# Scatters of routed rows spread over the batches, with a third buffer of rows and indices

## The chip, the cores and the metric

The kernel runs on one core of a Trainium2 chip. The metric is device time in microseconds of one execution, from three runs: 939.26, 940.46 and 940.62, median 940.46. A run with the hardware profiler on gives the trace that is read below.

## The reference

One decoder layer over 64 batches of 128 tokens with 128 features, in float32:

```python
x = src + linear_attention(layer_norm(src)); x = x + gelu(layer_norm(x) @ w1 + b1) @ w2 + b2
x = x + cross_attention(layer_norm(x), ctx)              # 16 heads of 8, 77 keys for each batch
probs = softmax(layer_norm(x) @ gate_w.T)                # 8 experts, each token takes the top 2
rank = cumsum(one_hot(top_i), axis=0) - 1                # rank of a token at its expert, over all 8192 tokens
keep = rank < capacity                                   # 1280 rows for each expert and choice
x = x + sum over kept choices of weight * down(silu(gate(z)) * up(z))   # z = layer_norm(x)
```

(Shortened: biases and the fill of masked keys are left out.)

## The kernel before

It has three stages. The first does linear attention and the feed-forward part. The second (`cross_attention_and_routing`, about 260 to 690 us) does cross-attention and finds for every token its two experts and a row in each. The third (`experts_and_combine`) loads the rows of one expert after another, computes, and scatters the results.

**Turns.** The second stage works on 16 groups of four batches (NG = 16, G4 = 4; a batch is one tile of 128 tokens). Every engine has its own hand-written program: a loop over turns g from 0 to 18, and in each turn four steps j = 0 to 3, one for each batch b = 4g + j. Work is pipelined over turns. In turn g TensorE does the attention of group g, the out-projection of group g-1 (`project_out`), the transposes of group g-1's normalised rows (`t4`, L1363), the gate of group g-2 and its ranks. Scores (L1303) and their maxima (`tops`, L933, two halves for each batch) run two batches ahead.

**GpSimd's steps.** For batch b+2 `split_top` (L811 and L813) writes the maxima as a high and a low part into Mx. TensorE transposes them one batch later (`turn_top`, L1308). `ln_scale` (L821 to L826) makes the scale and shift of the third norm for group g+2 in step 0 and of the fourth norm for group g-1 in step 2; `add_out_bias` (L831) follows in step 2. In between stand the scatters.

**Scatters.** `scatter_rows` (L834) is an indirect DMA: 128 rows of one tile, from z4 to the DRAM tensor `dispatched` of choice k, at the rows that `idx` holds. A row holds the normalised features, the residual and five numbers. Each group has four tiles and two choices, so eight scatters. In turn g, step 3, GpSimd waits for `residual_ready` and `idx_ready` of group g-2 and scatters tile 0 (both choices). In the next turn, tiles 1 and 2 go around the split of step 0 and tile 3 behind the split of step 1. For the last two groups (14 and 15) the first choice of all tiles goes first, then the second.

**Who waits for the scatters.** z4 and idx have two buffers. ScalarE (`ln4_apply`, L1197 and L1198, step 2) writes group g-1's rows and first waits until the scatters of group g-3 have landed. Behind it on ScalarE's queue stand the exponentials of the next batch (`exps`, L1215), for which TensorE waits before L1308. VectorE waits in step 13 of `route`. SyncE waits for all first-choice scatters before the first `load_x` (xin) of the third stage, and for all second-choice scatters before its second half.

**The order at the end.** Turns 14 and 15 have no third norm left to scale, turn 16 has no attention of its own, and its step 2 holds the fourth norm's scale of group 15.

Of the kernel before, what the change touches and what calls it, by code (L numbers as in the profile page):

```python
# [16 lines left out]
P = 128  # L17
# [26 lines left out]
NO_TOKEN = float(2 ** 20)  # L44
TOKENS = P * B


# [4 lines left out]
def some(count):  # L52

    return not isinstance(count, int) or count > 0
# [635 lines left out]
def cross_attention_and_routing(nc, ctx, sems, d, X, ident, neghalf, psum, banks, xg, c):  # L690
# [5 lines left out]
    if True:  # L696
        def sb(name, shape, dt=F32):
            return ctx.enter_context(nc.sbuf_tensor(name, shape, dt))

        def sem(name):  # L700
# [29 lines left out]
        var4, rs4, shift4 = (sb(n, [P, G4]) for n in ("var4", "rs4", "shift4"))  # L730
        z4 = [sb(f"z4{i}", [P, G4, ROW]) for i in range(2)]
        z4T = sb("z4T", [P, G4 * P])
# [10 lines left out]
        rank, row, drop = (sb(n, [P, G4, K2]) for n in ("rank", "row", "drop"))  # L743
        idx = [sb(f"idx{i}", [P, G4, K2], I32) for i in range(2)]

# [4 lines left out]
                 "ln4_stats ln4_moments ln4_var ln4_rstd ln4_shift z4_ready z4T_ps z4T_ready gate_ps dl_ready ex_ready "  # L750
                 "rank_ps ranked_ready residual_ready idx_ready step scattered0_0 scattered1_0 scattered0_1 scattered1_1").split()
        s = {n: sem("b_" + n) for n in names}
# [38 lines left out]
        def gpsimd(pool):  # L791
# [40 lines left out]

            def scatter_rows(par, t, k):
                pool.indirect_dma_start(xg[k], bass.IndirectOffsetOnAxis(ap=idx[par][:, t, k:k + 1], axis=0), z4[par][:, t, :], None,  # L834
                                        bounds_check=E * CAP - 1, oob_is_err=False).then_inc(s[f"scattered{par}_{k}"], 16)

            def scatter(g, par, t):
                if t == 0:
                    pool.wait_ge(s["residual_ready"], g + 1)
                    pool.wait_ge(s["idx_ready"], g + 1)  # L840
                    pool.sem_inc(s["passed"], 1)
                if not isinstance(g, int) or g < NG - 2:
                    for k in range(K2):
                        scatter_rows(par, t, k)

                elif t == 0:
                    for u in range(G4):
                        scatter_rows(par, u, 0)
                elif g == NG - 2:
                    if t == 1:  # L850
                        scatter_rows(par, 0, 1)
                        scatter_rows(par, 1, 1)
                else:
                    for u in range(2):
                        if t == 1:
                            scatter_rows(1 - par, 2 + u, 1)
                        else:
                            scatter_rows(par, 2 * (t - 2) + u, 1)

            def steps(g, par):  # L860
                other = 1 - par
                for j in range(G4):
                    b = G4 * g + j
                    if j == 0:
                        if group(g + 2):
                            ln_scale(g + 2, 3, mom3, var3, rs3, shift3)
                        if group(g - 3):
                            scatter(g - 3, other, 1)
                    if j == 2:
                        if group(g - 1):  # L870
                            ln_scale(g - 1, 4, mom4, var4, rs4, shift4)
                        if group(g):
                            add_out_bias(g)
                    if batch(b + 2):
# [33 lines left out]
        def vector(dve):  # L908
# [85 lines left out]
            def route(g, par, k):  # L994
# [44 lines left out]
                if k == 13:  # L1039
                    if some(g - 1):  # L1040
                        for k in range(K2):
                            dve.wait_ge(s[f"scattered{par}_{k}"], 16 * G4 // 2 * (g - par))

                    v.tensor_scalar(taken[:], rank[:, :, 1], float(CAP), None, ALU.is_lt)
                    v.tensor_scalar(z4[par][:, :, ALONE], rank[:, :, 1], float(CAP), None, ALU.is_ge)
# [6 lines left out]
                if k == 15:  # L1052
                    v.tensor_tensor(z4[par][:, :, PLACE], away[:], codes[:, bass.ts(g, G4)], ALU.add)
                    ins = v.reciprocal(z4[par][:, :, WEIGHT], pair[:])
                if k == 16:
                    ins = v.tensor_tensor(z4[par][:, :, WEIGHT + 1], z4[par][:, :, WEIGHT], ex[:, :, E], ALU.mult)
                ins.then_inc(s["step"], 1)

            def indices(g, par):
                dve.wait_ge(s["step"], STEPS * g + STEPS)  # L1060
                v.scalar_tensor_tensor(idx[par][:], row[:], float(ROWS), drop[:], ALU.add, ALU.add).then_inc(s["idx_ready"], 1)

# [118 lines left out]
        def scalar(act):  # L1181
# [7 lines left out]

            def ln4_apply(g, par, t):  # L1190
                if t == 0:
                    act.wait_ge(s["ln4_shift"], g + 1)
                    if some(g - 1):
# [3 lines left out]
                    nc.scalar.activation(z4[par][:, :, CODE:CODE + 1], codes[:, bass.ts(g, G4)].unsqueeze(2), ACT.Copy)  # L1197
                ins = nc.scalar.activation(z4[par][:, t, 0:P], xrow(g, t), ACT.Identity, bias=shift4[:, t:t + 1], scale=rs4[:, t:t + 1])  # L1198
                if t == G4 - 1:
                    ins.then_inc(s["z4_ready"], 1)  # L1200
# [6 lines left out]

            def residual_side(g, par):
                nc.scalar.activation(z4[par][:, :, X_AT:X_AT + P], X[:, bass.ts(g, G4), :], ACT.Copy).then_inc(s["residual_ready"], 1)

# [25 lines left out]
            def steps(g, par):  # L1236
                other = 1 - par
                for j in range(G4):
                    b = G4 * g + j
                    if batch(b):  # L1240
                        exps(b, j)
                    if batch(b - 1):
                        num_out(b - 1)
                    if batch(b + 1):
                        MT_side(b + 1)
                    if j == 1 and group(g + 2):
                        ln3_apply(g + 2)
                    if j == 2:
                        if group(g - 2):
                            gate_exps(g - 2)  # L1250
                        if group(g - 1):
                            for t in range(G4):
                                ln4_apply(g - 1, other, t)
                    if j == 3 and group(g - 1):
                        z4T_side(g - 1)
                        residual_side(g - 1, other)

# [16 lines left out]
        def tensor(pe):  # L1274
# [84 lines left out]

            def t4(g, par):  # L1360
                pe.wait_ge(s["z4_ready"], g + 1)
                for t in range(G4):
                    last = nc.tensor.transpose(misc[:, t * P:(t + 1) * P], z4[par][:, t, 0:P], ident[:])  # L1363
                last.then_inc(s["z4T_ps"], 1)
# [19 lines left out]
            def steps(g, par):  # L1384
# [3 lines left out]
                for j in range(G4):  # L1388
# [47 lines left out]
                    if j == 3 and group(g - 1):  # L1436
                        if group(g + 2):
                            pe.wait_ge(s["z3T_ready"], g + 3)
                        else:
                            pe.wait_ge(s["ranked_ready"], g - 1)  # L1440
                        t4(g - 1, other)

# [58 lines left out]
def experts_and_combine(nc, ctx, sems, d, X, ident, psum, banks, xg, out):  # L1501
# [6 lines left out]
    if True:  # L1508
# [54 lines left out]
        def sync(sp):  # L1563
            def load_x(n, i, p):
# [4 lines left out]
                if n == SECOND:  # L1569
                    for par in (0, 1):  # L1570
                        sp.wait_ge(b[f"scattered{par}_1"], 16 * G4 * NG // 2)
                slot = n // SECOND
# [45 lines left out]
            for g in range(NG - 2, NG):  # L1618
                store_x(g)
            for par in (0, 1):  # L1620
                sp.wait_ge(b[f"scattered{par}_0"], 16 * G4 * NG // 2)
            load_x(0, 0, 0)
# [222 lines left out]
```

## Time and profile before

| | |
|---|---|
| Median of three runs | 940.46 us |
| The profiled execution | 943.81 us, of which the span of the trace is 942.0 us |
| TensorE busy | 860.0 us, 91% of the span |
| VectorE busy | 652.4 us, 69% |
| GpSimd busy | 538.7 us, 57% |
| ScalarE busy | 449.4 us, 48% |
| Scatters of the second stage (L834) | 128, busy 129.5 us, mean 1012 ns |
| GpSimd idle ahead of L811, waiting for the maxima | 108.6 us, 36 times |

Engines in rows: PE is TensorE's matmuls, PEld its weight loads, DVE VectorE, ACT ScalarE, POOL GpSimd, SP SyncE; a q behind a name is the engine's sequencer. Matmuls overlap and their ends are modelled. Ln is line n of the kernel. An arrow `out<-in` names tiles by the program's names without their numbers; "z" stands for z4 too. A releaser in square brackets is what ended the idle time before an instruction. "issue" means that the profile shows nothing it waited for.

### The profile page before, as it was taken

What the parts mean: (1) busy time and instruction counts of PE and PEld (TensorE: products, weight loads), DVE (VectorE), ACT (ScalarE), POOL (GpSimd) and SP (SyncE); (2) the same over time, 40 slices, a digit from 0 to 9 for tenths busy, and PEclk for the clock granted to TensorE, in tenths of its full rate; (3) what the DMA queues carried; (4) which work ended last, traced back from release to release, by engine and by line L of the source; (5) the groups of instructions that cost most, each with busy time, mean ns of one, the idle gap of its engine ahead of it and who ended that gap; (6) DMA issues with size and microseconds to landing.
All of it is one profiled execution on the core that took longest, in us unless ns stands there. A gap on an engine that the chain in (4) does not pass through costs nothing.

```text
span 942.0 us, 25271 instructions
## 1 busy us (share of the span) xinstructions
PE 860.0 (91%) x9107; PEld 614.8 (65%) x9107; DVE 652.4 (69%) x2060; ACT 449.4 (48%) x695; POOL 538.7 (57%) x747
## 2 busy tenths in 40 slices
PE   3799999999989999999999999997449999989994
PEld 2577777777656666666666666665327777657672
DVE  5789989999736688888888888764415555464553
ACT  1267566675435666666666666654122223322330
POOL 3356666566432236656666666653646666657775
PEclk9799999999989999999999999987569999999997
DMA  7269930000000001111000000010143545456660
GB/s 242 89 233 403 402 152 0 0 0 2 1 1 2 14 26 59 59 60 41 32 28 29 31 29 29 30 47 24 39 149 110 159 126 157 121 173 194 197 196 7
DMA packets 50335, 86.99 MB, mean 92 GB/s; under 512 B 12809, under 2 KB 28105, under 8 KB 50232
## 3 DMA queue, kind: packets, MB, share of 16 engines
q1 hardware_dynamic: 37872, 72.18, 22.6%
q0 software_dynamic: 11264, 12.70, 4.2%
q8 instruction: 66, 1.08, 0.5%
q10 hardware_dynamic: 1096, 0.73, 0.2%
q14 instruction: 37, 0.30, 0.1%
HBM read 42.08 MB, written 58.41 MB: 107 GB/s over the span
## 4 chain that ended last, share of the span: by engine, by line
PE 50%; POOL 7%; issue 6%; DVE 5%; ACT 5%; DMA 2%; POOLq 0%; SPq 0%; DVEq 0%; ACTq 0%
PE psum L1743 14%; PE psum L1755 7%; PE psum L1303 6%; PE psum L1317 4%; PE psum L1337 4%; POOL dispatched L834 3%; ACT PT L1215 2%; PE psum L1737 2%; ACT z L1198 2%; PE psum L1357 2%; PE psum L1345 2%; PE psum L1287 1%; POOL rs L824 1%; PE psum L1370 1%; PE psum L625 1%
## 5 line engine op out<-in xcount | busy, mean ns | idle before, releaser
L1642 POOL DMA_INDIRECT out<-yo,token x160 | 157.6, 985 | 82.8 <-issue 70.4
L834 POOL DMA_INDIRECT dispatched<-z,idx x128 | 129.5, 1012 | 68.5 <-issue 68.5
L1215 ACT ACTIVATE PT<-psum,key_bias 77x2048 f32<-77x2048 f32 x64 | 125.5, 1960 | 78.8 <-PE psum L1320 78.8
L1724 ACT ACTIVATE act_g<-psum 128x512 f32<-128x512 f32 x80 | 47.3, 597 | 159.7 <-PE psum L1743 137.5
L933 DVE TENSOR_REDUCE top_score<-psum 128x8 f32<-128x616 f32 x128 | 101.4, 792 | 29.1 <-PE psum L1303 25.9
L1303 PE MATMUL psum<-Kb,qT 32*128 32x308 f32 x512 | 102.3, 475 | 0.4 <-DVE top_score L933 0.4
L1680 DVE SCALAR_TENSOR_TENSOR yo<-psum,xin,base 128x128 f32<-128x128 f32 x156 | 44.0, 344 | 75.7 <-PE psum L1755 75.4
L1317 PE MATMUL psum<-qT,Kb 32*77 32x128 f32 x2048 | 86.7, 285 | 0.1
L1755 PE MATMUL psum<-down,h 128*128 128x128 f32 x640 | 78.3, 275 | 4.0 <-DVE h L1695 4.0
L1755 PEld LDWEIGHTS psum<-down,h 128*128 128x128 f32 x640 | 74.7, 192 | 5.8 <-DVE h L1695 5.3
L1743 PE MATMUL psum<-xT,gate 128*128 128x512 f32 (+1 forms) x192 | 77.1, 532 | 0.8 <-ACT xT L1715 0.8
L1743 PE MATMUL psum<-xT,up 128*128 128x512 f32 (+1 forms) x192 | 75.4, 522 | 0.0
L811 POOL CAST Mx<-top_score 128x16 bf16<-128x16 f32 x64 | 12.9, 201 | 108.6 <-DVE top_score L933 108.6
L1337 PE MATMUL psum<-PT,V 77*32 77x128 f32 x2048 | 70.9, 280 | 0.7 <-issue 0.7
L1337 PEld LDWEIGHTS psum<-PT,V 77*32 77x32 f32 x2048 | 53.3, 111 | 27.4 <-issue 27.0
L1317 PEld LDWEIGHTS psum<-qT,Kb 32*77 32x77 f32 x2048 | 60.6, 146 | 11.6 <-issue 11.0
L625 PE MATMUL psum<-w,hT 128*128 128x128 f32 x512 | 66.8, 281 | 0.8 <-ACT hT L522 0.8
L1695 DVE TENSOR_TENSOR h<-psum,act_g 128x512 f32<-128x512 f32 x80 | 54.0, 686 | 15.5 <-PE psum L1743 15.5
L625 PEld LDWEIGHTS psum<-w,hT 128*128 128x128 f32 x512 | 62.6, 197 | 1.6 <-ACT hT L522 1.6
L605 PE MATMUL psum<-ln2T,w 128*128 128x512 f32 x128 | 61.8, 605 | 0.6
L1320 PE MATMUL psum<-MT,minus_sel 32*77 32x128 bf16 x1024 | 61.0, 217 | 0.0
L1743 PEld LDWEIGHTS psum<-xT,gate 128*128 128x128 f32 x192 | 36.9, 193 | 33.5 <-issue 31.8
(173 smaller groups left out, 1744.5 us busy)
## 6 DMA issues: line engine op xcount, KB each, us to landing
dispatched<-zeros SPq DMA_DIRECT2D x40, 522.0 KB, 6.5
xin<-dispatched SPq DMA_DIRECT2D x40, 522.0 KB, 3.6
out<-zeros SPq DMA_DIRECT2D x20, 256.0 KB, 3.1
first<-out SPq DMA_DIRECT2D x20, 256.0 KB, 4.3
X<-in_x SPq DMA_DIRECT2D x16, 256.0 KB, 2.6
out<-X SPq DMA_DIRECT2D x16, 256.0 KB
out<-yo,token POOLq DMA_INDIRECT x160, 2.7
ctx<-in_ctxT SPq DMA_DIRECT2D x4, 616.0 KB, 5.8
```

Source lines behind the costliest of these rows:

```text
L605: nc.tensor.matmul(h_ps[c % 2], w1[:, c * P:(c + 1) * P], ln2T[:], start=True, stop=True).then_inc(s["h_ps"], 1)
L625: last = nc.tensor.matmul(w2_ps[:, t, :], hT[:, c, t * P:(t + 1) * P], w2[:, c, :], start=(c == 0), stop=(c == FC - 1))
L834: pool.indirect_dma_start(xg[k], bass.IndirectOffsetOnAxis(ap=idx[par][:, t, k:k + 1], axis=0), z4[par][:, t, :], None, bounds_check=E * C ...
L933: v.tensor_reduce(top_score[p][:, 2 * HB * half:2 * HB * half + 2 * HB], S, AX.X, ALU.max).then_inc(s["top_ready"], 1)
L1215: nc.scalar.activation(PT[j % 2][:], T.rearrange("p a c -> p (a c)"), ACT.Exp, bias=key_bias[:, bass.ds(b, 1)]).then_inc(s["PT_ready"], 1)
L1303: nc.tensor.matmul(S[:, i], qT[par][rows_of(q), j * P:(j + 1) * P], Kb[par][rows_of(q), :, j * S2:(j + 1) * S2], start=True, stop=True).th ...
L1317: nc.tensor.matmul(T[:, q, h * P:(h + 1) * P], Kb[par][rows_of(q), h, j * S2:(j + 1) * S2], qT[par][rows_of(q), j * P:(j + 1) * P], start= ...
L1320: last = nc.tensor.matmul(T[:, q, h * P:(h + 1) * P], minus_sel[rows_of(q), h, :], MT[rows_of(q), :], start=False, stop=True)
L1337: last = nc.tensor.matmul(pv[rows_of(q), a * P:(a + 1) * P], V[par][:, (H // 2) * j + x, ROWS_Q * i:ROWS_Q * i + ROWS_Q], PT[j % 2][:, (2 ...
L1642: pool.indirect_dma_start(rows_out if slot else out, bass.IndirectOffsetOnAxis(ap=token[i][:, t:t + 1], axis=0), yo[i][:, t, :], None, bou ...
L1743: last = nc.tensor.matmul(target[c][:, a:b], weights[which][:, c * P:(c + 1) * P], xT[i][:, a:b], start=True, stop=True)
L1755: last = nc.tensor.matmul(target, h[:, c, t * P:(t + 1) * P], down[which][:, c, :], start=(c == 0), stop=(c == HC - 1))
```

## The change

z4 and idx get three buffers (Z4 = 3); which one a group uses is g mod 3, and every wait on a buffer's scatters counts by it. Groups 0 to 13 are scattered one tile in each step, three turns behind (n = g-3): the wait for group n's residual and indices moves from step 3 of turn n+2 to step 0 of turn n+3; then in each step GpSimd waits for the first half of batch b+2's maxima, scatters the first choice of tile j, splits the maxima, and scatters the second choice. Groups 14 and 15 keep their order. The scales and the out-bias stay where they were within the steps.

```diff
+Z4 = 3
-        z4 = [sb(f"z4{i}", [P, G4, ROW]) for i in range(2)]
+        z4 = [sb(f"z4{i}", [P, G4, ROW]) for i in range(Z4)]
-        idx = [sb(f"idx{i}", [P, G4, K2], I32) for i in range(2)]
+        idx = [sb(f"idx{i}", [P, G4, K2], I32) for i in range(Z4)]
...
+            def scatter_ready(g):
+                pool.wait_ge(s["residual_ready"], g + 1)
+                pool.wait_ge(s["idx_ready"], g + 1)
+                pool.sem_inc(s["passed"], 1)
...
             def steps(g, par):
-                other = 1 - par
                 for j in range(G4):
                     b = G4 * g + j
-                    if j == 0:
-                        if group(g + 2):
-                            ln_scale(g + 2, 3, mom3, var3, rs3, shift3)
-                        if group(g - 3):
-                            scatter(g - 3, other, 1)
+                    n = g - 3
+                    paced = 0 <= n < NG - 2
+                    if j == 0 and group(g + 2):
+                        ln_scale(g + 2, 3, mom3, var3, rs3, shift3)
                     if j == 2:
                         if group(g - 1):
                             ln_scale(g - 1, 4, mom4, var4, rs4, shift4)
                         if group(g):
                             add_out_bias(g)
+                    if paced:
+                        if j == 0:
+                            scatter_ready(n)
+                        if batch(b + 2):
+                            pool.wait_ge(s["top_ready"], 2 * (b + 2) + 1)
+                        scatter_rows(n, j, 0)
+                    elif j < G4 - 1 and group(n):
+                        scatter_last(n, j + 1)
                     if batch(b + 2):
                         split_top(b + 2, j % 2)
-                    if j == 3 and group(g - 2):
-                        scatter(g - 2, par, 0)
-
-                    if j < 2 and group(g - 3):
-                        scatter(g - 3, other, j + 2)
+                    if paced:
+                        scatter_rows(n, j, 1)
+                    if j == 3 and g - 2 in (NG - 2, NG - 1):
+                        scatter_last(g - 2, 0)
...
-                    if some(g - 1):
-                        act.wait_ge(s["z4T_ps"], g - 1)
+                    if some(g // Z4):
+                        act.wait_ge(s["z4T_ps"], g - Z4 + 1)
                         for k in range(K2):
-                            act.wait_ge(s[f"scattered{par}_{k}"], 16 * G4 // 2 * (g - par))
+                            act.wait_ge(s[f"scattered{g % Z4}_{k}"], 16 * G4 * (g // Z4))
```

The wait of VectorE in step 13 of `route` and SyncE's waits change in the same way. `scatter_last` issues for groups 14 and 15 what `scatter` issued for them.

## Rows read from the trace of the kernel before

**Rows 1.** Stretches of TensorE: span, busy (instructions), granted clock, DMA share, GB/s

```profile
405.00:429.00 24.00, 23.70 (x425) 1.00 0.14 50
...
453.00:547.00 94.00, 93.81 (x1624) 1.00 0.09 28
...
626.00:628.00 2.00, 0.79 (x13) 1.00 0.00 0
628.00:630.00 2.00, 2.00 (x11) 0.60 0.00 0
...
640.00:642.00 2.00, 2.00 (x38) 0.50 0.00 0
```

**Rows 2.** Timeline of TensorE: start, us, operation, tiles, count, idle time before

```profile
556.54 0.23 PE L1308 MATMUL psum<-ident_b,Mx 128*128 128x128 bf16 x1
...
559.09 1.12 PE L1287 MATMUL psum<-z3T,wq 128*128 128x512 f32 x2
...
561.87 0.79 PE L1283 MATMUL psum<-ctx,wk 128*128 128x308 f32 x2
...
565.85 0.66 PE L1351 MATMUL psum<-ident,o 128*128 128x128 f32 x4
...
627.98 0.23 PE L1308 MATMUL psum<-ident_b,Mx 128*128 128x128 bf16 x1 [1.14 <-ACT PT L1215]
...
641.56 0.88 PE L1351 MATMUL psum<-ident,o 128*128 128x128 f32 x4
```

**Rows 3.** Timelines of VectorE and ScalarE in turn 14, step 2

```profile
620.79 0.36 DVE L926 BATCH_NORM_AGGREGATE mom<-stat 128x2 f32<-128x6 f32 x4
...
624.32 0.21 ACT L1197 ACTIVATE z<-codes 128x4 f32<-128x4 f32 x1 [1.63 <-DMA dispatched<-z,idx]
```

**Rows 4.** Timeline of GpSimd in turn 14, steps 1 and 2

```profile
620.82 0.98 POOL L834 DMA_INDIRECT dispatched<-z,idx  x1 [0.30 <-issue]
621.88 0.25 POOL L821 TENSOR_SCALAR minus_mean<-mom 128x4 f32<-128x4 f32 x1
...
623.62 0.20 POOL L826 TENSOR_TENSOR shift<-minus_mean,rs 128x4 f32<-128x4 f32 x1
623.77 1.26 POOL L831 TENSOR_TENSOR xb<-X,bo_row 128x512 f32<-128x512 f32 x1
...
625.26 0.23 POOL L813 TENSOR_TENSOR Mx<-top_score,Mx 128x16 bf16<-128x16 f32 x1
```

**Rows 5.** Timelines of GpSimd and VectorE from turn 16 on, then the chain

```profile
671.67 0.20 POOL L826 TENSOR_TENSOR shift<-minus_mean,rs 128x4 f32<-128x4 f32 x1
...
676.11 0.98 POOL L834 DMA_INDIRECT dispatched<-z,idx  x1 [1.96 <-issue]
...
682.82 0.17 DVE L1061 SCALAR_TENSOR_TENSOR idx<-row,drop 128x8 int32<-128x8 f32 x1
...
687.69 2.11 DMA dispatched<-z,idx
689.86 4.55 DMA xin<-dispatched
```

**Rows 6.** Timelines of GpSimd, VectorE and ScalarE in turn 15, step 2

```profile
650.78 0.25 POOL L821 TENSOR_SCALAR minus_mean<-mom 128x4 f32<-128x4 f32 x1
...
648.92 0.38 DVE L926 BATCH_NORM_AGGREGATE mom<-stat 128x2 f32<-128x6 f32 x4 [0.18 <-DVE stat L917]
...
652.79 0.21 ACT L1197 ACTIVATE z<-codes 128x4 f32<-128x4 f32 x1 [2.28 <-POOL shift L826]
```

**Rows 7.** The page's group of L811: busy, mean ns, idle before

```profile
L811 POOL CAST Mx<-top_score 128x16 bf16<-128x16 f32 x64 | 12.9, 201 | 108.6 <-DVE top_score L933 108.6
```

**Rows 8.** Timelines of VectorE and GpSimd in a steady turn

```profile
549.21 0.69 DVE L963 COPY V<-psum 77x512 f32<-77x512 f32 x1
...
548.54 1.00 POOL L834 DMA_INDIRECT dispatched<-z,idx  x1 [0.51 <-issue]
...
560.29 1.13 POOL L834 DMA_INDIRECT dispatched<-z,idx  x1 [1.24 <-issue]
```

More of the change, by code:

```diff
@@ L750, in cross_attention_and_routing @@
                  "ln4_stats ln4_moments ln4_var ln4_rstd ln4_shift z4_ready z4T_ps z4T_ready gate_ps dl_ready ex_ready "
-                 "rank_ps ranked_ready residual_ready idx_ready step scattered0_0 scattered1_0 scattered0_1 scattered1_1").split()
+                 "rank_ps ranked_ready residual_ready idx_ready step scattered0_0 scattered1_0 scattered2_0 scattered0_1 scattered1_1 scattered2_1").split()
         s = {n: sem("b_" + n) for n in names}
@@ L831, in add_out_bias, with scatter_rows, scatter_last @@
                 pool.tensor_tensor(xb[:], X[:, bass.ts(g, G4), :], over(bo_row[:], 1, G4), ALU.add).then_inc(s["xb_ready"], 1)
[L833 to L837, printed above, removed]
-                if t == 0:
[L839 to L846, printed above, removed]
+            def scatter_rows(n, t, k):
+                pool.indirect_dma_start(xg[k], bass.IndirectOffsetOnAxis(ap=idx[n % Z4][:, t, k:k + 1], axis=0), z4[n % Z4][:, t, :], None,
+                                        bounds_check=E * CAP - 1, oob_is_err=False).then_inc(s[f"scattered{n % Z4}_{k}"], 16)
+            def scatter_ready(g):
+                pool.wait_ge(s["residual_ready"], g + 1)
+                pool.wait_ge(s["idx_ready"], g + 1)
+                pool.sem_inc(s["passed"], 1)
+            def scatter_last(n, t):
+                if t == 0:
+                    scatter_ready(n)
                     for u in range(G4):
-                        scatter_rows(par, u, 0)
-                elif g == NG - 2:
+                        scatter_rows(n, u, 0)
+                elif n == NG - 2:
                     if t == 1:
-                        scatter_rows(par, 0, 1)
-                        scatter_rows(par, 1, 1)
+                        scatter_rows(n, 0, 1)
+                        scatter_rows(n, 1, 1)
                 else:
@@ L1060, in indices @@
                 dve.wait_ge(s["step"], STEPS * g + STEPS)
-                v.scalar_tensor_tensor(idx[par][:], row[:], float(ROWS), drop[:], ALU.add, ALU.add).then_inc(s["idx_ready"], 1)
+                v.scalar_tensor_tensor(idx[g % Z4][:], row[:], float(ROWS), drop[:], ALU.add, ALU.add).then_inc(s["idx_ready"], 1)
             def steps(g, par):
@@ L1188, in ln3_apply, with ln4_apply @@
                 ins.then_inc(s["z3_ready"], 1)
-            def ln4_apply(g, par, t):
+            def ln4_apply(g, t):
                 if t == 0:
                     act.wait_ge(s["ln4_shift"], g + 1)
-                    if some(g - 1):
-                        act.wait_ge(s["z4T_ps"], g - 1)
+                    if some(g // Z4):
+                        act.wait_ge(s["z4T_ps"], g - Z4 + 1)
                         for k in range(K2):
-                            act.wait_ge(s[f"scattered{par}_{k}"], 16 * G4 // 2 * (g - par))
-                    nc.scalar.activation(z4[par][:, :, CODE:CODE + 1], codes[:, bass.ts(g, G4)].unsqueeze(2), ACT.Copy)
-                ins = nc.scalar.activation(z4[par][:, t, 0:P], xrow(g, t), ACT.Identity, bias=shift4[:, t:t + 1], scale=rs4[:, t:t + 1])
+                            act.wait_ge(s[f"scattered{g % Z4}_{k}"], 16 * G4 * (g // Z4))
+                    nc.scalar.activation(z4[g % Z4][:, :, CODE:CODE + 1], codes[:, bass.ts(g, G4)].unsqueeze(2), ACT.Copy)
+                ins = nc.scalar.activation(z4[g % Z4][:, t, 0:P], xrow(g, t), ACT.Identity, bias=shift4[:, t:t + 1], scale=rs4[:, t:t + 1])
                 if t == G4 - 1:
@@ L1252, in steps @@
                             for t in range(G4):
-                                ln4_apply(g - 1, other, t)
+                                ln4_apply(g - 1, t)
                     if j == 3 and group(g - 1):
                         z4T_side(g - 1)
-                        residual_side(g - 1, other)
+                        residual_side(g - 1)
             def between(g, place):
@@ L1358, in project_out, with t4 @@
                 last.then_inc(s["out_ps"], 1)
-            def t4(g, par):
+            def t4(g):
                 pe.wait_ge(s["z4_ready"], g + 1)
                 for t in range(G4):
-                    last = nc.tensor.transpose(misc[:, t * P:(t + 1) * P], z4[par][:, t, 0:P], ident[:])
+                    last = nc.tensor.transpose(misc[:, t * P:(t + 1) * P], z4[g % Z4][:, t, 0:P], ident[:])
                 last.then_inc(s["z4T_ps"], 1)
@@ L1440, in steps @@
                             pe.wait_ge(s["ranked_ready"], g - 1)
-                        t4(g - 1, other)
+                        t4(g - 1)
                     if batch(b + 1):
@@ L1569, in load_x @@
                 if n == SECOND:
-                    for par in (0, 1):
-                        sp.wait_ge(b[f"scattered{par}_1"], 16 * G4 * NG // 2)
+                    for i3 in range(Z4):
+                        sp.wait_ge(b[f"scattered{i3}_1"], 16 * G4 * ((NG - 1 - i3) // Z4 + 1))
                 slot = n // SECOND
@@ L1619, in sync @@
                 store_x(g)
-            for par in (0, 1):
-                sp.wait_ge(b[f"scattered{par}_0"], 16 * G4 * NG // 2)
+            for i3 in range(Z4):
+                sp.wait_ge(b[f"scattered{i3}_0"], 16 * G4 * ((NG - 1 - i3) // Z4 + 1))
             load_x(0, 0, 0)
```

19 lines of the change are left out of this document (10 added, 9 removed).

## The prediction

> **What bounds the kernel now.** I read the page's slices first: TensorE is full nearly everywhere, except around 625 to 695 us, where its share and its clock both fall. The stretches then say what is at stake [rows 1]. [...] From 405 to 429 there are 0.30 us of idle time, the largest of a steady turn. [...]
>
> TensorE's own rows show it [rows 2]. The transpose of batch 60's maxima (L1308) starts at 627.98 after 1.14 us of idle time that ScalarE's exponentials ended. The work from there to L1351 takes 641.56 - 627.98 = 13.58 us. In a steady turn the same distance is 565.85 - 556.54 = 9.31 us and holds two steps that turn 14 no longer has, the query and key projections (L1287, L1283). Their starts to the next instruction are 1.05 and 0.72 us (their rows last 1.12 and 0.79, with 0.07 of overlap at each end). So the work is 7.54 us at the full clock, and the fall of the clock cost 6.04 us.
>
> Why were the exponentials late? ScalarE first applies the fourth norm (L1197, L1198). It waited 1.63 us for that, and the profile names a scatter as releaser [rows 3]. GpSimd's rows [rows 4] show two causes almost on top of each other: the second scatter of tile 3 of group 11 is issued at 620.82 and ScalarE starts at 624.32; and behind the same scatters stands the norm's scale (L821 to L826), which begins at 621.88 and ends at 623.82, though the moments were ready at 620.79 + 0.36 = 621.15 [rows 3]. ScalarE needs both: z4 has two buffers, so group 13 writes where group 11 is still being read.
>
> Last I read the tail. Routing of group 15 is a chain through all engines, and its first-choice scatters open the expert stage: the last of them starts at 687.69, lands 2.11 us later, and the load of xin takes 4.55 us more [rows 5].
>
> **The change part by part.** *Third buffer.* After the change ScalarE and VectorE wait for scatters three groups back, which under the new order end a turn before. That wait is gone (I count it at nothing remaining). Next late in turn 14 is the scale. After batch 59's split only one scatter stands ahead of it instead of two, so GpSimd is free 1.3 us sooner, but the moments at 621.15 now bound it. I allow 0.22 us from the moments to the start; then it starts at 621.37, ends at 623.31 (duration 623.82 - 621.88 = 1.94, [rows 4]) and ScalarE starts at 623.35 instead of 624.32: 0.97 us earlier. TensorE's idle time shrinks from 1.14 to 0.17 us, less than the 0.30 us that the turn at 405 had with the clock kept at 1.00 [rows 1]. I therefore take the clock to stay up: 6.04 us more. Bounds: 0 (it falls all the same) and 6.04.
>
> *Turn 15.* The same step again [rows 6]: scale at 650.78, though moments were ready at 648.92 + 0.38 = 649.30. With one scatter fewer it starts at 649.52, 1.26 us earlier, and ScalarE, which waited 2.28 us for it with nothing else to do, follows by the whole 1.26 us; the exponentials of the last batch and all behind them are on the path. Bounds 0.5 and 1.3.
>
> *Steady turns.* TensorE's idle time is at most what can be won: 0.19 us in four turns of 453 to 547, about 0.05 in each, and 0.30 in the one at 405 [rows 1]. Over some twelve turns this is 0.9 us. Bounds 0 and 1.5.
>
> *The new place of the first-choice scatter.* It stands ahead of the split of a batch's maxima and waits for their first half. The split itself waits for the second half, and ahead of it GpSimd sat idle for 108.6 us over the whole stage, 1.7 us for each of the 64 splits [rows 7]. The scatter fills this. The exception is the third batch of a turn, where scale and out-bias (L831) come first. For turn 14: shift ends at 623.31; the bias sum ends 1.21 us later (in the trace 625.03 against 623.82), 624.52; a scatter has a gap of 0.51 before it and lasts 1.00 to 1.13 [rows 8], so it ends at 626.03 to 626.16; the two instructions of the split take 0.46 (from the bias sum's end, 625.03, to 625.49, [rows 4]). Mx is ready at 626.5 to 626.6, and TensorE asks for it at 627.0. It fits, by 0.4 to 0.5 us, so I cost it at nothing. Without that cover every excess is paid in all of about twelve turns, since TensorE sets them. The added waits (semaphores alone) are hidden in the same way. What is queued behind the wait for the first half is only the split, which waits for the second half anyway.
>
> The scatter now runs beside other VectorE work. Beside the copy of V (0.69 us) a scatter lasted 1.00 us, no more than one in the tail where VectorE is mostly idle, 0.98 [rows 5, 8]. [...]
>
> *The tail.* This part loses. Group 13's eight scatters used to run before the last scale (L821 at turn 16). Now two tiles go before and two behind it, and the latter stand in the same queue ahead of groups 14 and 15. Before: shift ends at 671.87 and the last first-choice scatter starts at 687.69, so 15.82 us [rows 5]. In it lie an idle stretch of 1.96 us and a wait for group 15's indices, which VectorE writes by 682.99. After: 4 scatters of group 13, then 4 and 2 of group 14, then 4 of group 15. The fourteenth starts 0.51 + 1.43 + 12 x 1.28 = 17.30 us behind shift: 0.51 is the gap ahead, 1.13 + 0.30 the first, 0.98 + 0.30 each further one [rows 4, 8]. Each of two new groups adds 0.73, as the gap ahead of a group's first scatter is 1.24 against 0.51 [rows 8]: 18.76 us. The indices no longer bound it, as the queue reaches group 15 at about 685.5. Cost: 18.76 - 15.82 = 2.9 us. Lower bound 1.5 (the two 0.73 hidden), upper 4.6 (the unexplained gap of 1.96 in the place of 0.3 comes again). Second-choice scatters end some 3 us later too, ahead of the first scatter of the expert stage, which needs its first projection: nothing.
>
> **Sum.** -0.97 - 6.04 - 1.26 - 0.9 + 2.9 = -6.3 us. The profiled execution took 943.81 us (span 942.0), which gives 937.5. The median of the runs shown is 940.46, 3.35 lower, so on that basis 934.2.
>
> **The rivals.** *A, the clock falls all the same*, or the timed runs, unlike the profiled one, never had the fall. Then 6.04 us drop out: -0.97 - 1.26 - 0.9 + 2.9 = -0.2, so 940.3; with the tail's upper bound 941.9. For it: a short gap remains and TensorE has less and less to do from turn 14 on; 3.35 us between profile and median are not explained. Against it: the steady turns keep the clock with gaps like the remaining one, and the three runs lie within 1.4 us, less than a fall that comes and goes would give. Chance 0.16, a quarter of it beyond 0.2% slower.
>
> *B, slower: the maxima's split comes late.* Place: third batch of each turn, first-choice scatter ahead of L811. It decides once gap and scatter together take more than about 2.0 us instead of 1.6; the gap of 1.96 us in [rows 5] is an example of one that would. At 0.5 us late in each of twelve turns it costs 6 us, turn 14 keeps its idle time and its slow clock, and the tail adds 2.9, less the 1.26 of turn 15: about 948. For it: the margin is only 0.4 to 0.5 us. Against it: the gap of 1.24 us is the longer kind [rows 8], and it stands ahead of a group's first scatter, which is not this place. Chance 0.06.
>
> *C, the tail costs little.* If the two 0.73 are hidden the cost is 1.5, and the steady turns may give their 1.5: 934.2 - 1.4 - 0.6 = 932.2; each microsecond by which the clock stays up longer in turn 16 takes up to another half: 930 to 932. Chance 0.05.
>
> **How the numbers follow.** The forecast (934.2) has 0.72; its own range, from the bounds of steady turns, turn 15 and tail, is 931.5 to 937. The range for 8 in 10 must take in A's middle and C: 930.5 to 941.5. About 0.2% (1.9 us) is what a measurement of this kernel can tell from no change. Faster: 0.72 + 0.05 = 0.77; same: 0.12 of A and 0.01 of cases not named, 0.13; slower: B, the rest of A, 0.10.
>
> **What would show it.** In the trace of after: ScalarE's L1197 waits for the shift alone, never for a scatter; in turn 14 the scale starts about 0.2 us behind the moments and L1308 has under 0.3 us of idle time; the granted clock stays at 1.00 from 626 to beyond 642; the last L1308 of a steady turn never waits for Mx. In the tail, four scatters stand between L826 and group 14's, and some 18.7 us lie between the last shift and the last first-choice scatter. The prediction fails if the clock row at 628 is 0.50 again, if L1308 waits for L813, or if the tail grows by more than 5 us.

## The result, and the profile after

The kernel after took 931.55 us (median of four runs, 930.51 to 932.49) against 940.54 (939.26 to 941.46): a ratio of 0.9905, 95% interval 0.9888 to 0.9922, 9.0 us less. Two further comparisons (e5 and e12, the kernel after unchanged; e5 was expected at 930.5 to 933 us) took 932.21 and 933.53 us and gave 0.9895 (0.9869 to 0.9921) and 0.9907 (0.9885 to 0.9930). The forecast was 934.2, or 6.3 us less than before.

TensorE's stretches of the kernel after (columns as in [rows 1]) show the main point. Turn 14 ends at about 622 here, and the clock no longer falls behind it:

```profile
610.00:620.00 10.00, 10.00 (x193) 1.00 0.27 85
620.00:630.00 10.00, 9.70 (x196) 1.00 0.09 29
630.00:640.00 10.00, 9.05 (x211) 1.00 0.14 47
640.00:645.00 5.00, 2.41 (x42) 0.81 0.07 22
```

The timelines of GpSimd, ScalarE and TensorE in turn 14 answer to [rows 4], [rows 3] and [rows 2]:

```profile
614.21 1.00 POOL L835 DMA_INDIRECT dispatched<-z,idx  x1 [0.51 <-issue]
616.08 0.24 POOL L822 TENSOR_SCALAR minus_mean<-mom 128x4 f32<-128x4 f32 x1 [0.87 <-DVE mom L930]
...
617.82 0.20 POOL L827 TENSOR_TENSOR shift<-minus_mean,rs 128x4 f32<-128x4 f32 x1
617.97 1.27 POOL L832 TENSOR_TENSOR xb<-X,bo_row 128x512 f32<-128x512 f32 x1
619.42 1.11 POOL L835 DMA_INDIRECT dispatched<-z,idx  x1 [0.18 <-issue]
620.54 0.20 POOL L812 CAST Mx<-top_score 128x16 bf16<-128x16 f32 x1
...
618.05 0.21 ACT L1201 ACTIVATE z<-codes 128x4 f32<-128x4 f32 x1 [0.67 <-POOL shift L827]
...
620.75 0.66 PE L1367 MATMUL psum<-ident,z 128*128 128x128 f32 x4
621.71 0.23 PE L1312 MATMUL psum<-ident_b,Mx 128*128 128x128 bf16 x1 [0.29 <-ACT PT L1219]
```

GpSimd now waits 0.87 us for the moments, where it used to be 0.7 us late for them. TensorE's idle time ahead of its L1312 (L1308 before) is 0.29 us instead of 1.14. Mx is written 0.6 us ahead of it (the second instruction of the split starts at 620.84 and lasts 0.25). Over the whole trace ScalarE's L1201 (L1197 before) waits 16 times, each time for the shift, and never for a scatter.

TensorE's timeline of a steady turn has the transposes of two successive batches' maxima at these places before, where the next one is the 556.54 of [rows 2], and then after:

```profile
550.98 0.22 PE L1308 MATMUL psum<-ident_b,Mx 128*128 128x128 bf16 x1
```

```profile
546.43 0.22 PE L1312 MATMUL psum<-ident_b,Mx 128*128 128x128 bf16 x1
551.78 0.22 PE L1312 MATMUL psum<-ident_b,Mx 128*128 128x128 bf16 x1
```

5.56 us before, 5.35 after, and the three other steps of the turn are unchanged to 0.01 us. ScalarE's exponentials, in its timeline before and then after, say why:

```profile
554.53 1.95 ACT L1215 ACTIVATE PT<-psum,key_bias 77x2048 f32<-77x2048 f32 x1
```

```profile
549.49 1.95 ACT L1219 ACTIVATE PT<-psum,key_bias 77x2048 f32<-77x2048 f32 x1
```

Before, they end at 556.48, 0.06 us ahead of L1308, so TensorE was waiting for them; after, they end at 551.44, 0.34 us ahead of L1312. This distance from one L1308 to another is the yardstick of everything below. It gives a ladder of stretches for each profiled execution, in us (b is the batch whose transpose starts or ends the stretch; the last shift and the scatter count by their starts; the first expert is TensorE's first transpose of xin):

| Profiled execution | start to b 3 | b 3 to 59 | 59 to 60 | 60 to 62 | 62 to last shift | to last first-choice scatter | to first expert | rest |
|---|---|---|---|---|---|---|---|---|
| before | 292.79 | 329.16 | 6.03 | 17.11 | 26.58 | 16.02 | 6.76 | 247.52 |
| after | 290.20 | 326.44 | 5.07 | 10.93 | 25.54 | 17.43 | 6.58 | 246.50 |
| before, again (e1) | 292.62 | 329.02 | 6.19 | 14.00 | 26.53 | 16.02 | 6.48 | 246.75 |
| after, again (e5) | 292.49 | 326.44 | 5.06 | 10.94 | 25.57 | 17.50 | 6.36 | 246.83 |
| after, third (e12) | 293.02 | 326.45 | 5.06 | 10.94 | 25.64 | 17.52 | 6.59 | 247.03 |

The two spans first compared differ by 13.3 us, more than the 9.0 of the medians. The first column accounts for 2.6 of it: the first 45 us have a mean granted clock of 0.85 in the trace of before and of 0.92 in that of after, and this varies for one and the same kernel (0.92, 0.85 and 0.85 in the three profiles of the kernel after, whose first column is 290.20, 292.49 and 293.02). The last column adds 1.0, about what it varies by itself (246.75 to 247.52 before, 246.50 to 247.03 after). What the change did stands between them: -2.7, -1.0, -6.2 (-3.1 against e1), -1.0 and +1.4.

The timed runs narrow down the third of these. Each has its granted clock, as a mean over the execution. In the 51 runs of the kernel before that ran beside the experiments up to e12 it lies between 0.951 and 0.961, median 0.955, and one run of them reaches 0.960; in the 16 of the kernel after it lies between 0.956 and 0.964, median 0.960, and only one is below 0.960. The share of the clock that was not granted, times the time, is 42.4 us in the median before and 37.3 after. So an estimate of what the clock gave back in a typical run is 5.1 us. The mean does not say where in an execution the clock was low; the profiles say that.

### The profile page after: what moved, and what is told of

The parts are those of the page before. It is cut to its first block, busy times and chain, and to the rows that moved or that the text cites. A ratio compares the mean times of both kernels' runs of the same rounds, so it can differ in the third digit from the quotient of the medians.

```text
span 928.7 us, 25269 instructions
## 1 busy us (share of the span) xinstructions
PE 849.0 (91%) x9107; PEld 609.0 (66%) x9107; DVE 648.7 (70%) x2060; ACT 450.6 (49%) x695; POOL 537.0 (58%) x747
## 4 chain that ended last, share of the span: by engine, by line
PE 66%; DVE 3%; issue 2%; POOL 2%; ACT 1%; DMA 1%; POOLq 0%; DVEq 0%; SPq 0%; ACTq 0%
PE psum L1747 14%; PE psum L1307 9%; PE psum L1759 8%; PE psum L1321 7%; PE psum L1341 7%; PE psum L1349 2%; PE psum L1361 2%; PE psum L1741 2%; PE psum L1291 2%; PE psum L1295 2%; PE psum L1374 2%; PE psum L626 1%; PE psum L1324 1%; PE psum L1287 1%; PE psum L606 1%
## 5 line engine op out<-in xcount | busy, mean ns | idle before, releaser
L1321 PE MATMUL psum<-qT,Kb 32*77 32x128 f32 x2048 | 84.6, 280 | 0.1
```

The source lines that it names most:

```text
L1321: nc.tensor.matmul(T[:, q, h * P:(h + 1) * P], Kb[par][rows_of(q), h, j * S2:(j + 1) * S2], qT[par][rows_of(q), j * P:(j + 1) * P], start= ...
```

## The experiments

**The fall of the clock in turn 14: does it recur (e1)?** The kernel before, unchanged.

> The kernel before, unchanged, looked at once more. My theory (the 1.14 us of idle time ahead of L1308 in turn 14 makes the clock fall) expects the same gap of 1.1 to 1.2 us and the granted clock at 0.5 for 10 to 14 us behind it, and 939 to 942 us. The rival (the fall was an accident of that one execution) expects the gap but the clock at 1.00 from 620 to 650 us, and then some 934 us.

939.42 us, from one run. TensorE's timeline and then its stretches:

```profile
626.07 0.63 PE L1363 MATMUL psum<-ident,z 128*128 128x128 f32 x4 [0.25 <-ACT z L1198]
627.83 0.23 PE L1308 MATMUL psum<-ident_b,Mx 128*128 128x128 bf16 x1 [1.14 <-ACT PT L1215]
```

```profile
628.00:632.00 4.00, 4.00 (x57) 0.57 0.00 0
632.00:635.00 3.00, 2.99 (x51) 1.00 0.14 44
635.00:638.00 3.00, 3.00 (x48) 0.54 0.12 35
```

The gap is the same to the hundredth, and the clock fell again, but for twice 3.4 us and not for the 10 to 14 that I expected: the two batches behind took 14.00 us and not 17.11 (10.93 at the full clock). The gap belongs to the kernel; the length of the fall behind it varies. The other profiled execution had a clock of 0.953, one of the lower ones.

**Buffer or order (e2, e10)?** e2 keeps the third buffer and puts back the order of before (shortened here):

```diff
...
-                    if paced:
-                        scatter_rows(n, j, 1)
-                    if j == 3 and g - 2 in (NG - 2, NG - 1):
-                        scatter_last(g - 2, 0)
+                    if j == 3 and group(g - 2):
+                        scatter(g - 2, 0)
+                    if j < 2 and group(g - 3):
+                        scatter(g - 3, j + 2)
```

> The third buffer alone, the scatters in the order of the kernel before. Theory one (the order of GpSimd's queue does it): the scale of group 13 still begins 0.7 us behind the moments; ScalarE starts 0.4 us earlier in turn 14, the idle time ahead of L1308 is 0.65 to 0.75 us, the steady turns keep 23.63 us, turn 15 gains nothing. If that gap still lets the clock fall, 939.5 to 940.5 us; if not, 933.5 to 934.5. Rival (the buffer does it): 931 to 932.5 us, nothing left for the order.

935.53 us, ratio 0.9953 (0.9936 to 0.9971). GpSimd's, ScalarE's and TensorE's timelines in turn 14:

```profile
619.08 0.98 POOL L835 DMA_INDIRECT dispatched<-z,idx  x1 [0.30 <-issue]
620.13 0.25 POOL L822 TENSOR_SCALAR minus_mean<-mom 128x4 f32<-128x4 f32 x1
...
622.11 0.21 ACT L1198 ACTIVATE z<-codes 128x4 f32<-128x4 f32 x1 [1.16 <-POOL shift L827]
...
625.76 0.23 PE L1309 MATMUL psum<-ident_b,Mx 128*128 128x128 bf16 x1 [0.78 <-ACT PT L1216]
```

The scale still starts right behind the scatters, but ScalarE no longer waits for their landing. The gap of 0.78 us stands near the expected 0.65 to 0.75, and the clock stayed at 1.00; the seven timed runs have 0.960 or 0.961. The time is 1.0 us above the range expected for that case. So half of what the step lost (6.03 to 5.55 us) comes from the buffer and half (5.55 to 5.07) from the order on top of it, and in these runs the first half sufficed for the clock. The steady turns kept their length (328.67 against 329.02 and 329.16), and turn 15 gained nothing (26.90). Neither theory had it alone. The order with two buffers was not run.

e10 has one tile in each step, as the kernel after, but both choices behind the split:

```diff
-                        if batch(b + 2):
-                            pool.wait_ge(s["top_ready"], 2 * (b + 2) + 1)
-                        scatter_rows(n, j, 0)
...
                     if paced:
+                        scatter_rows(n, j, 0)
                         scatter_rows(n, j, 1)
```

> The kernel after, one tile in each step, but both choices behind the split and without the wait for the first half of the maxima. Theory (what counts is how much stands ahead of the scale): two scatters stand between step 1's split and the scale again, so steady turns of 23.6 us, the scale of turn 14 about 0.7 us behind the moments, idle time there of 0.7 to 0.8 us, sometimes a fall of the clock; 934.5 to 938 us. Rival (the even spreading is what helps): steady turns of 23.4 us and 931.5 to 933 us.

937.83 us, ratio 0.9967 (0.9948 to 0.9986). Steady stretch 328.56, step 59 to 60 5.55, gap 0.78 us: the same as e2 to about 0.1 us. The even spreading does nothing for the turns by itself, and it brings the longer tail (17.49 us against 15.99 in e2). The profiled execution shows no fall, but four of the ten timed runs have a mean clock of 0.956 or 0.957 and take 939.5 to 940.5 us, and five have 0.960 to 0.962 and 934.6 to 937.2. So a gap of 0.78 us may not be safe in each execution; where the clock was low in those four isn't recorded.

**One place of the order (e3).** Third buffer, the order of before, but the two scatters of tile 3 behind the scale (the lines that differ from e2):

```diff
-                    if j < 2 and group(g - 3):
+                    if j < 2 and group(g - 3) and (j == 0 or g - 3 >= NG - 2):
                         scatter(g - 3, j + 2)
+                    if j == 2 and 0 <= g - 3 < NG - 2:
+                        scatter(g - 3, 3)
```

> Third buffer, the order of before but for one place: tile 3 of groups 0 to 13 goes behind the split of step 2, and with it behind the fourth norm's scale, instead of ahead of it. Theory one (what counts is how much stands ahead of the scale): steady turns of 23.4 us as in the kernel after, the clock stays up in turn 14, and in the tail only two scatters stand behind the last scale instead of four, so the last first-choice scatter is bound by group 15's indices: 930.0 to 931.5 us, as fast as the kernel after or up to 1.4 us faster. Rival (the scatter ahead of the split and the spreading over four steps matter): 934 us or more.

933.46 us, ratio 0.9922 (0.9902 to 0.9941). Steady stretch 326.44, turn 14 5.06 and 10.94, tail 15.96: each as expected, every stretch up to the experts at least as good as in the kernel after but for 0.3 to 0.4 us ahead of the last shift. The time was 2 us above the expectation all the same; the rest took 248.67 us, of which below. What the order wins in the second stage is thus won by what stands ahead of the fourth norm's scale.

**The gap as the cause (e6, e7, e9b).** Spare sums on GpSimd, writing tiles that nothing reads, ahead of the scale in one turn (the tiles' allocation is left out here):

```diff
                     if j == 2:
+                        for spare_i in spare if g == 14 else ():
+                            pool.tensor_tensor(spare_i[:], over(bo_row[:], 1, G4), over(bo_row[:], 1, G4), ALU.add)
                         if group(g - 1):
```

> The kernel after with two spare sums of 1.27 us each on GpSimd ahead of the fourth norm's scale, in turn 14 only; they write tiles that nothing reads. GpSimd has 0.87 us of idle time there, so the scale comes some 1.7 us later. Theory (the idle time ahead of L1308 makes the clock fall): 2.0 us idle, the clock at 0.5 for 3 to 14 us behind it, the two batches behind it take 2 to 7 us longer, 935 to 940 us. Rival (the clock fell for another reason that the change happens to remove): the time grows by the 1.7 us alone, 932.5 to 934 us, clock 1.00 until 640.

943.39 us, ratio 1.001 (0.9975 to 1.0045), above the expected 935 to 940: two instructions in one turn undo the whole change. TensorE's timeline, then its stretches:

```profile
623.32 0.63 PE L1370 MATMUL psum<-ident,z 128*128 128x128 f32 x4 [0.39 <-ACT z L1205]
625.08 0.29 PE L1315 MATMUL psum<-ident_b,Mx 128*128 128x128 bf16 x1 [1.13 <-ACT PT L1222]
```

```profile
625.00:630.00 5.00, 4.92 (x57) 0.50 0.07 22
630.00:640.00 10.00, 10.00 (x104) 0.50 0.04 14
640.00:645.00 5.00, 5.00 (x45) 0.50 0.07 22
```

The step grew by 1.27 us and the two batches behind it took 19.98 us instead of 10.94. Against e5 nothing else in the ladder moved by more than 0.7. The ten timed runs fall into two bands: three take 935.5 to 936.5 us at a mean clock of 0.956 to 0.960, seven take 941.7 to 948.4 at 0.942 to 0.952. So with the same gap the fall stays away or nearly so in some executions and is longer than the profiled one in others.

> The same two spare sums in turn 8, where TensorE has a full load on both sides. Theory (idle time of this length lowers the clock wherever it lies): 1.4 to 1.7 us idle ahead of L1308 of turn 8, the clock at 0.5 for 3 to 14 us, 935 to 940 us. Rival (only where TensorE has less and less to do): 1.5 us more and no fall, 932.5 to 934 us.

The same sums in turn 8 left only 0.66 us idle, not 1.4 to 1.7; my estimate of the cover there was wrong. No fall, 933.11 us (ratio 0.9908, 0.9881 to 0.9936), so it told nothing about longer gaps. The time alone would mislead here: against e5 the stretch ahead of the last shift was 1.5 us shorter and the rest 1.4 us longer. Three sums (e9) have no result: with the third spare tile, `hT` no longer fitted into SBUF (it needs 8192 B, and 6432 were left). I added a power of 1.04 us to the two:

```diff
+                        if g == 8:
+                            pool.tensor_tensor(tiny[:], open_inv[:, 0:G4], neghalf[:, 0:G4], ALU.pow)
```

> The kernel after with two spare sums of 1.27 us and one spare power of 1.04 us (a [128, 4] tile) ahead of the fourth norm's scale in turn 8; nothing reads their results. Two sums alone left 0.66 us idle ahead of L1308 there with the clock unmoved. Now 1.7 to 1.8 us, longer than the 1.14 us that went with a fall in turn 14. Theory (idle time of this length lowers the clock in a full turn too): the clock at 0.5 for 3 to 20 us from about 483 us on, 1.1 us more than with two sums from the gap and 3 to 10 from the clock, at least in some executions: 936 to 944 us. Rival (it takes the thinner work of turn 14): 934 to 935 us and no fall.

Timeline and stretches of TensorE in turn 8:

```profile
484.57 0.63 PE L1373 MATMUL psum<-ident,z 128*128 128x128 f32 x4 [0.47 <-issue]
486.33 0.29 PE L1318 MATMUL psum<-ident_b,Mx 128*128 128x128 bf16 x1 [1.14 <-ACT PT L1225]
```

```profile
483.00:486.20 3.20, 1.73 (x38) 0.98 0.04 12
486.50:492.50 6.00, 6.00 (x57) 0.50 0.10 31
493.50:500.00 6.50, 6.50 (x111) 1.00 0.02 4
```

The clock fell for 6.8 us in the middle of full turns. The step behind took 9.76 us; in this trace the same step of the neighbouring turns takes 7.3, in the others 6.76, so the clock cost 2.4 to 3.0 us. A fall needs no thinner work as in turn 14. The times can't be compared with the others. On this chip the kernel before took 1016.77 us and this variant 988.98 (ratio 0.9718, 0.9663 to 0.9773), its rest (the last column of the ladder) took 288 us, and the first step of most turns 0.57 us more. The change, with a handicap on top, is worth 28 us there instead of 9. Nothing in this account explains that, and there is no trace of the kernel before from that chip.

**Rival B's price (e8).** One spare sum between the first-choice scatter and the split, third batch of each turn:

```diff
+                    if paced and j == 2 and batch(b + 2):
+                        pool.tensor_tensor(spare[g % 2][:], over(bo_row[:], 1, G4), over(bo_row[:], 1, G4), ALU.add)
                     if batch(b + 2):
                         split_top(b + 2, j % 2)
```

> The kernel after with one spare sum of 1.27 us on GpSimd between the first-choice scatter and the split in the third batch of each turn: the price of my rival B. In the trace of after Mx was written 0.95 us ahead of L1308, so the split should now be 0.3 to 0.5 us late in each of eleven turns: L1308 waits for L813's successor there, steady turns of 23.7 to 23.9 us, 935 to 938 us. If the cover were larger than the trace says: no change, 931.5 us.

939.12 us, ratio 0.9951 (0.9927 to 0.9976), 1.1 us above the expected range. Ten steady turns grew by 0.20 us each and turn 8 by 0.7, in sum 2.76 (329.20). In turn 14 TensorE waited for Mx itself, and the clock fell:

```profile
627.35 0.22 PE L1315 MATMUL psum<-ident_b,Mx 128*128 128x128 bf16 x1 [0.81 <-POOL Mx L815]
```

```profile
628.00:632.00 4.00, 4.00 (x58) 0.57 0.08 28
632.00:635.00 3.00, 2.99 (x48) 1.00 0.09 28
635.00:638.00 3.00, 3.00 (x51) 0.52 0.06 18
```

The cover is real: 1.27 us more takes it away. The steady turns lost less than I expected (0.3 to 0.5), the clock added 3.1. The nine timed runs fall into two bands here too: 933.3 to 936.0 us at 0.960 to 0.964, and 939.1 to 943.2 at 0.954 to 0.957.

**The tail (e4, e11).** Group 13's scatters all in steps 0 and 1 of turn 16, ahead of the last scale (shortened here):

```diff
+                    if n == NG - 3:
+                        if j == 0:
+                            scatter_ready(n)
+                        for u in (2 * j, 2 * j + 1) if j < 2 else ():
+                            for k in range(K2):
+                                scatter_rows(n, u, k)
+                        paced = False
...
```

> The kernel after, but group 13's eight scatters all go in steps 0 and 1 of turn 16, ahead of the last scale. GpSimd idled 5.9 us ahead of that scale and the four scatters take 5.1, so they fit. Theory (the tail's 1.4 us come from these four): the last first-choice scatter starts about 16.0 us behind the last shift instead of 17.2, and the time is 1.0 to 1.4 us lower, 930.1 to 930.6. Rival (the tail is bound by the indices or by the load of xin): no change against the kernel after, 931.5.

> Group 13's scatters ahead of the last scale once more, now beside the kernel after on the same chip. The last first-choice scatter starts 16.0 us behind the last shift against 17.5. If that is all, the time is 1.0 to 1.5 us below the kernel after. The rival (the same 1.4 us are given back in the third stage, where the trace of the first look showed 2 to 3 us more around its middle): within 0.5 us of it.

> The kernel after, unchanged, as the partner of the tail variant. 930.5 to 933.5 us. The stretch from the first expert's transposes to the end took 246.5 and 246.8 us in the two looks so far; if the third stage's middle falls one way or the other by chance, values up to 250 should come up here too.

The stretch itself behaves: 16.01 and 16.02 us instead of 17.43 to 17.52. The time does not: 933.20 us beside 933.53 for the kernel after on the same chip (ratios to before 0.9914 and 0.9907, the intervals overlap almost wholly), and 933.61 in e4, where I had expected 930.1 to 930.6. Both profiles give it back in the rest: 249.89 and 249.79 us, against 246.50 to 247.03 in the three profiles of the kernel after. At about 827 us, where the second choices begin, VectorE waits for the load of `first` (2.75 us in e12) and TensorE for VectorE's `h`. In e11 and e4 the instructions behind that wait ran at a slow clock (0.50 over 826 to 828 us in e11 and over 828 to 830 in e4; 1.00 over 828 to 832 in e12). TensorE's timelines of e12 and then e11:

```profile
827.70 2.05 PE L1759 MATMUL psum<-down,h 128*128 128x128 f32 x16 [2.55 <-DVE h L1699]
```

```profile
825.73 3.53 PE L1766 MATMUL psum<-down,h 128*128 128x128 f32 x16 [2.48 <-DVE h L1706]
...
861.94 2.05 PE L1766 MATMUL psum<-down,h 128*128 128x128 f32 x16 [0.50 <-DVE h L1706]
```

A gap of 2.5 us stands in both; one lowered the clock and the other not. Instruction by instruction, e11 loses 0.6 us against e12 in the first transposes of the third stage, some 1.4 at 827 (3.53 against 2.05 us), and 0.7 in a second wait for `h` ahead of 861.94 that e12 does not have. e2, e3 and e7 show the same fall at 825 to 829 (the 16 instructions take 3.45 to 3.51 us, the rest 248.07 to 248.67); among the profiles other than e9b's it stands in five and not in eight. The timed runs speak for more than chance: nine of the twelve of e4 and e11 have a mean clock of 0.958 or 0.959, against 0.960 or more in 15 of the 16 of the kernel after. Why this order should bring the fall about is open. No variant that I ran beats the kernel after.

## Why the prediction was right, and where not

**The clock of turn 14** carried the sum (6.04 us, worked out from [rows 1] and [rows 2]) and is shown: with the gap at 0.29 to 0.30 us the clock stayed at 1.00 in all three profiles, and a gap of 1.13 and 1.14 us made by spare instructions brought the fall to 0.50 back (e6, e9b). Its size was 6.2 us against the first trace, 3.1 against e1, and about 5.1 by the mean clocks of the timed runs. The term was too large for a typical run: it was read from one execution with a longer fall than most. That also bears on the 3.35 us between profile and median, which I had left unexplained.

**The gap of turn 14**: forecast 0.97 us, measured 0.96 (6.03 to 5.07). The idle time that remains is 0.29 us and not 0.17, because not all of the 0.96 was idle time ahead of L1308. TensorE's row ahead of it, before:

```profile
626.21 0.63 PE L1363 MATMUL psum<-ident,z 128*128 128x128 f32 x4
```

From there to the transpose of Mx it is 1.77 us before (627.98) and 0.96 after (621.71 - 620.75), so 0.81 less. The other 0.15 lay ahead of L1363, which reads what ScalarE's norm writes and was late with it. My view that the scale was late on its own, behind the scatter's landing, holds: e2 took the landing away and left half.

**Steady turns**: the step that was wrong. I bounded the gain by TensorE's idle time, 0.05 us in each turn, at most 1.5 in all. It was 2.7 us, in eleven turns: 0.20 to 0.21 in seven of them, 0.3 to 0.45 in three, 0.04 in one. The ends of matmuls are modelled, so a short wait does not show as idle time. In the turn shown above all 0.21 lie between the start of the last instruction of L1363 and that of L1308: 0.32 us before (556.22 to 556.54) and 0.11 after, while that instruction's row is given 0.27 us.

**Turn 15**: forecast 1.26, measured 1.0 (26.58 to 25.54). GpSimd waited for the moments there too, and the scale came 1.26 us earlier, as forecast. Ahead of the last group's moments, VectorE then stands idle for 0.53 us instead of 0.17; the trace doesn't say what for.

**The tail**: forecast 2.9, measured 1.4, below my lower bound's 1.5 by a hair. The part that I counted scatter by scatter was right: 17.30 us from the end of the last shift, measured 17.23. The term that was wrong is the 0.73 us for each of two new groups. GpSimd's timeline of after, from the last scale on:

```profile
658.18 0.20 POOL L827 TENSOR_TENSOR shift<-minus_mean,rs 128x4 f32<-128x4 f32 x1
658.92 1.11 POOL L835 DMA_INDIRECT dispatched<-z,idx  x1 [0.54 <-issue]
660.34 0.97 POOL L835 DMA_INDIRECT dispatched<-z,idx  x1 [0.30 <-issue]
...
664.15 0.97 POOL L835 DMA_INDIRECT dispatched<-z,idx  x1 [0.31 <-issue]
...
671.79 0.97 POOL L835 DMA_INDIRECT dispatched<-z,idx  x1 [0.30 <-issue]
...
675.61 0.97 POOL L835 DMA_INDIRECT dispatched<-z,idx  x1 [0.30 <-issue]
```

664.15 and 671.79 are the first scatters of groups 14 and 15, with the ordinary gap of 0.30 us. With other scatters ahead of them in the queue, the waits and counters of a group added nothing to that gap. In e11 group 14's first scatter stands right behind the last scale, and the two longer gaps are back, though the profile names nothing that they waited for:

```profile
661.20 1.11 POOL L835 DMA_INDIRECT dispatched<-z,idx  x1 [1.17 <-issue]
664.08 0.98 POOL L835 DMA_INDIRECT dispatched<-z,idx  x1 [1.77 <-issue]
```

**The rivals.** A (no gain from the clock) did not come about. Its second form, that the timed runs never had the fall, is answered by their mean clocks: 50 of 51 before lie below 0.960. B did not come about; turn 14 left a margin of 0.6 us (the gap ahead of the scatter was 0.18 us there, not 0.51), and e8 shows that a late split would have cost 2.8 us from the turns and about 3 from the clock, not the 6 and 6 that I put down. I had spread GpSimd's 108.6 us of idle time over all 64 splits, 1.7 us each, but it stands ahead of only 36 of them. C, to which I gave 0.05, comes nearest: its 930 to 932 us hold the measured time, the hidden 0.73 us happened, and the steady turns gave even more than its 1.5. Its longer full clock in turn 16 did not happen: the clock fell (to 0.50) some 10.5 us behind the transpose of batch 62 in both kernels.

**The sum.** By the measured terms it is -0.96 - 3.1 to 6.2 - 1.0 - 2.7 + 1.4, so 6.4 to 9.5 us less, and 8.4 with the 5.1 of the typical run; the three comparisons gave 7.9 to 9.3. That the forecast of 6.3 came so near is in part luck: the clock was priced too high for a typical run, the steady turns too low and the tail too dear. My bounds of the single terms also give 932.2 to 937.6 us, and not the 931.5 to 937 that I wrote; the measured 931.55 is just outside them.

**Scatters beside VectorE.** A copy beside a scatter did not lengthen it. In the steady turn of the kernel after shown above, a copy of z3T from PSUM (549.66, 0.69 us) ran beside the first-choice scatter at 549.20 for 0.65 of that scatter's 1.11 us; the one of turn 14 (619.42) has no copy beside it and lasted 1.11 too. The copy of V in [rows 8] is weaker evidence than I made of it, since it began only 0.67 us into that scatter of 1.00 us.

## What to carry to other kernels

On a full engine, look for short waits in the distance between the same instruction of one turn and the next, not in the idle time that a profile with modelled ends shows (here 0.20 us and more in most turns, against 0.05 of idle time). Read a queue up to the instruction others wait for, and move what nobody waits for behind it: that was worth more here than spreading it evenly (the steady stretch took 326.44 us in e3 and 328.56 in e10). And when a trace has a fall of the clock in it, take a second profile before pricing it and look at the mean clock of each timed run, since here the gap repeated to a hundredth (1.14 us) and the fall did not (13.7 us, then twice 3.4).

## What the runs showed of the hardware

Ahead of the transpose of Mx in turns 14 and 8, TensorE's granted clock fell behind idle stretches of 1.13 to 1.14 us (with 0.25 to 0.47 us more just ahead of them, or under 0.1 in the first trace) in each of the four profiles that had one (before, e1, e6, e9b), and behind one of 0.81 us (e8); it stayed at 1.00 in the profiles with 0.78 (e2, e10), 0.66 (e7) and 0.29 to 0.30. Behind the 0.91 us ahead of batch 63's transpose it stayed at 1.00 too (649.85 before, 637.40 after). By the mean clocks, two of e6's ten timed runs had little or no fall behind the gap that cost the profiled one 9 us, and some of e10's may have had one behind 0.78. At the third stage's middle 2.48 us lowered it in e11 and 2.55 did not in e12. The time at a granted clock of 0.50 behind a gap of 1.13 to 1.14 us was 13.7 us in the first trace, twice 3.4 in e1, 6.8 in e9b and 20.5 in e6, although TensorE was full from the first instruction on. So in these profiles a gap of one microsecond cost its own length plus 2.4 to 9 us. That a busy engine stayed slow for as long as the 20.5 us of e6 I had not expected.
